# Who normalises the last two output tiles of a graph kernel's second layer norm: GpSimd and VectorE in place of ScalarE

## What is computed

```python
x = _layernorm(x + _L0_gnn_ref(x, adj, pairs, Wq, bq, Wk, bk), axis=-1)
x = _layernorm(x + _L1_gnn_ref(x, adj, weight, bias), axis=-1)   # adj @ (x @ weight) + bias

def _layernorm(x, axis=-1, eps=1e-05):
    m = jnp.mean(x, axis=axis, keepdims=True)
    v = jnp.var(x, axis=axis, keepdims=True)
    return (x - m) / jnp.sqrt(v + eps)
```

## Time and profile before

| what | value |
|---|---|
| median of 3 runs | 167.08 us (166.68 to 167.78) |
| profiled execution | 167.5 us, span 165.7 us |
| PE busy | 154.7 us (93%) |
| DVE busy | 125.5 us (76%) |
| ACT busy | 75.2 us (45%) |
| POOL busy | 69.2 us (42%) |
| TensorE granted clock, mean | 0.994 of full speed |

### The profile page before, as it was taken

How to read it: one execution, slowest core, us unless ns; L and a number is a source line. 1 busy time by engine, 2 the same in 40 slices (tenths; PEclk the granted TensorE clock), 3 DMA queues, 4 the chain that set the end, 5 groups by cost and what they waited for, 6 DMA issues and landing times.

```text
span 165.7 us, 2912 instructions
## 1 busy us (share of the span) xinstructions
PE 154.7 (93%) x1029; PEld 81.1 (49%) x1029; DVE 125.5 (76%) x391; ACT 75.2 (45%) x126; POOL 69.2 (42%) x83
## 2 busy tenths in 40 slices
PE   3999899999999999999999999998999999999950
PEld 3954344455444445444444485444655444444530
DVE  2885689996899998999578897888971268666681
ACT  5685649855864422874181362151213104342451
POOL 7787777777777777777107271000030000000000
PEclk9999999999999999999999999999999999999997
DMA  4999979998259999451004700000005962312233
GB/s 123 381 375 338 338 223 357 389 404 326 77 148 320 372 362 395 146 131 38 0 0 127 227 23 4 0 0 0 0 17 145 335 187 78 131 63 76 87 127 127
DMA packets 16232, 28.99 MB, mean 175 GB/s; under 512 B 4769, under 2 KB 5953, under 8 KB 16086
## 3 DMA queue, kind: packets, MB, share of 16 engines
q1 hardware_dynamic: 10742, 24.14, 41.6%
q10 hardware_dynamic: 3280, 3.07, 5.5%
q0 software_dynamic: 2192, 1.57, 3.8%
HBM read 19.83 MB, written 8.58 MB: 171 GB/s over the span
## 4 chain that ended last, share of the span: by engine, by line
PE 38%; DVE 24%; DMA 15%; issue 6%; ACT 6%; POOL 4%; SPq 3%; ACTq 0%; DVEq 0%
PE acc L1379 15%; PE acc L1467 13%; DMA stage<-in_adj_T 6%; DMA x_sb<-in_x 6%; POOL found L659 4%; DVE st L900 3%; PE tr L1467 3%; DMA found<-in_adj,top_i 3%; ACT adjT L702 2%; DVE hot L919 2%; DVE y L949 2%; PE tr L1421 2%; PE tr L1457 2%; SPq L546 1%; DVE x1s L963 1%
## 5 line engine op out<-in xcount | busy, mean ns | idle before, releaser
L651 POOL DMA_INDIRECT ed_adj<-in_adj,ed_idx x47 | 47.2, 1003 | 14.5 <-issue 14.0
L1379 PE MATMUL acc<-adjT,x1s 128*128 128x512 f16 (+1 forms) x240 | 49.0, 354 | 0.0
L1311 PE MATMUL acc<-xs,adjT 128*128 128x512 f16 (+1 forms) x176 | 40.2, 379 | 0.2 <-ACT xs L718 0.2
L1379 PEld LDWEIGHTS acc<-adjT,x1s 128*128 128x128 f16 x240 | 22.8, 98 | 21.0 <-issue 0.2
L1311 PEld LDWEIGHTS acc<-xs,adjT 128*128 128x128 f16 (+1 forms) x176 | 16.5, 98 | 19.2 <-ACT xs L718 0.7
L1467 PE MATMUL acc<-whl,xs 128*128 128x512 f16 (+1 forms) x108 | 23.8, 370 | 0.0
L1467 PEld LDWEIGHTS acc<-whl,xs 128*128 128x128 f16 x108 | 10.6, 98 | 11.8
L1311 PE MATMUL tr<-xs,adjT 128*128 128x512 f16 (+1 forms) x66 | 15.2, 379 | 0.0
L702 ACT CAST adjT<-stage 128x1408 f16<-128x1408 f32 x9 | 12.3, 1362 | 4.3 <-DMA stage<-in_adj_T 4.1
L755 ACT ACTIVATE xs<-acc 128x512 f16<-128x512 f32 (+1 forms) x12 | 6.4, 540 | 12.2 <-PE acc L1383 12.2
L690 POOL DMA_INDIRECT x_dram<-wraw,back_i x1 | 1.3, 1336 | 21.5 <-DVE wraw L1229 21.5
(11 more groups left out here) (279 smaller groups left out, 231.9 us busy)
## 6 DMA issues: line engine op xcount, KB each, us to landing
stage<-in_adj_T SPq DMA_DIRECT2D x9, 704.0 KB, 10.3
x_dram<-x_sb SPq DMA_DIRECT2D x10, 256.0 KB
x_sb<-in_x SPq DMA_DIRECT2D x3, 768.0 KB, 7.4
sums_dram<-y ACTq DMA_DIRECT2D x6, 256.0 KB
sums_dram<-xd ACTq DMA_DIRECT2D x5, 256.0 KB, 6.6
x_sb<-x_dram SPq DMA_DIRECT2D x1, 1280.0 KB, 12.3
out<-y SPq DMA_DIRECT2D x5, 256.0 KB, 2.0
stage<-in_adj_T SPq DMA_DIRECT2D x3, 384.0 KB, 5.8
```

The costliest lines, as they stand in the source:

```text
L651: nc.gpsimd.indirect_dma_start(out=ed_adj[0:EP, c:c + 1], out_offset=None, in_=adj_flat, in_offset=bass.IndirectOffsetOnAxis(ap=ed_idx[0:E ...
L1311: last = mm(sum_bank(i)[:, :], adjT[0:width[k], k, i * P:(i + 1) * P], xs[0:width[k], half, k, :], start=(k == 0 and half == 0), stop=(k = ...
L1379: mm(mix_bank(u)[:, 0:j - i], x1s[:, half, k, f * P:(f + 1) * P], adjT[:, k, i:j], start=(k == 0 and half == 0), stop=False)
```

## The change

Tile 9 is no longer normalised by ScalarE but by GpSimd, in one `tensor_scalar` over all 512 columns, as (y - mean) times the reciprocal. Tile 10 is normalised by VectorE alone, all 512 columns, in the same form. Neither needs the shift, so for these two tiles `scale_shift` gives way to `one_over`, a reciprocal alone. ScalarE still takes both roots, and still normalises tiles 0 to 8. The semaphores change with the work: SP waits for GpSimd before the DMA of tile 9, and both last DMAs wait for VectorE alone. The four buffers, the parts of the last tile and TensorE's program stay.

```diff
--- before.py
+++ after.py
@@ -40,7 +40,6 @@
 BACK_BEFORE = {0: 0, 1: 1, 5: 2, 6: 3}
 SPANS = [(0, 512), (512, 1024), (1024, N)]
 UNITS = KF * len(SPANS)
-HALF = H // 2
 LAST_PARTS = ((0, 320), (320, H))
 OUTS = 6
 EARLY = 2
@@ -253,7 +252,7 @@
         qk_read, change_ready, change_T, dT_hi, dT_lo = map(sem, ("qk_read", "change_ready", "change_T", "dT_hi", "dT_lo"))
         dS_done, right_hi, right_lo = map(sem, ("dS_done", "right_hi", "right_lo"))
         bias_row_loaded, bias_split, biased, ones_laid, out_done, z_ready, z_moments, z_root = map(sem, ("bias_row_loaded", "bias_split", "biased", "ones_laid", "out_done", "z_ready", "z_moments", "z_root"))
-        z_stats, z_normed, z_half_normed = map(sem, ("z_stats", "z_normed", "z_half_normed"))
+        z_stats, z_normed, next_to_last, next_to_last_normed, last_normed = map(sem, ("z_stats", "z_normed", "next_to_last", "next_to_last_normed", "last_normed"))
 
         map_clear, map_idx_ready, map_zeroed, map_marked = map(sem, ("map_clear", "map_idx_ready", "map_zeroed", "map_marked"))
         general_in, rows_in, general_step, early_read = map(sem, ("general_in", "rows_in", "general_step", "early_read"))
@@ -603,10 +602,12 @@
                     sp.dma_start(x_sb[0:LAST, a, :], rows(x1_dram, a)).then_inc(x1_back[n], 16)
             unless_few(sp, "sp", slots_wanted(sp), ahead, general_sp)
             for n, t in enumerate(OUT_ORDER[:-1]):
-                sp.wait_ge(z_normed, n + 1)
+                if n < T - 2:
+                    sp.wait_ge(z_normed, n + 1)
+                else:
+                    sp.wait_ge(next_to_last_normed, 1)
                 sp.dma_start(rows(out, t), y4(n)[0:width[t]]).then_inc(out_stored[n % 4], 16)
-            sp.wait_ge(z_normed, T)
-            sp.wait_ge(z_half_normed, 1)
+            sp.wait_ge(last_normed, 1)
             sp.dma_start(rows(out, OUT_ORDER[-1])[0:64, :], y4(T - 1)[0:64, :]).then_inc(last_stored[0], 16)
             for b in range(4):
                 sp.wait_ge(out_stored[b], 16 * len(range(b, T - 1, 4)))
@@ -692,6 +693,9 @@
                 in_=q[0:SLOTS, :], in_offset=None, bounds_check=N - 1, oob_is_err=False).then_inc(x1_scattered, 16)
             pool.wait_ge(x1_scattered, 16)
             unless_few(pool, "pool", slots_wanted(pool), ahead, general_pool)
+            t = T - 2
+            pool.wait_ge(next_to_last, 1)
+            nc.gpsimd.tensor_scalar(y4(t), y4(t), st[:, t % 2, 6:7], st[:, t % 2, 8:9], ALU.subtract, ALU.mult).then_inc(next_to_last_normed, 1)
 
 
         @block.scalar
@@ -807,12 +811,11 @@
             for t in range(T):
                 act.wait_ge(z_moments, t + 1)
                 root(st[:, t % 2], eps[:]).then_inc(z_root, 1)
-                act.wait_ge(z_stats, t + 1)
-                part = y4(t) if t < T - 1 else y4(t)[:, 0:HALF]
-                nc.scalar.activation(part, part, ACT.Identity, bias=st[:, t % 2, 9:10],
-                                     scale=st[:, t % 2, 8:9]).then_inc(z_normed, 1)
-            act.wait_ge(z_normed, T)
-            act.wait_ge(z_half_normed, 1)
+                if t < T - 2:
+                    act.wait_ge(z_stats, t + 1)
+                    nc.scalar.activation(y4(t), y4(t), ACT.Identity, bias=st[:, t % 2, 9:10],
+                                         scale=st[:, t % 2, 8:9]).then_inc(z_normed, 1)
+            act.wait_ge(last_normed, 1)
             act.dma_start(rows(out, OUT_ORDER[-1])[64:P, :], y4(T - 1)[64:P, :]).then_inc(last_stored[1], 16)
 
 
@@ -904,6 +907,10 @@
 
                 step(V.reciprocal(s[:, 8:9], s[:, 10:11]))
                 return V.tensor_scalar(s[:, 9:10], s[:, 6:7], -1.0, s[:, 8:9], ALU.mult, ALU.mult)
+
+            def one_over(s):
+
+                return V.reciprocal(s[:, 8:9], s[:, 10:11])
 
             def hot_part(n):
 
@@ -1273,14 +1280,14 @@
                 if n == 0:
                     ins.then_inc(dve_step, 1)
                     steps += 1
-                    finish_stats(T - 2)
+                    dve.wait_ge(z_root, T - 1)
+                    one_over(st[:, (T - 2) % 2]).then_inc(next_to_last, 1)
             step(ins)
             dve.wait_ge(z_normed, t - 1)
             V.bn_aggr(st[:, t % 2, 6:8], last_st[:, 0:12]).then_inc(z_moments, 1)
-            finish_stats(t)
-            dve.wait_ge(z_stats, T)
-            part = y4(t)[:, HALF:H]
-            V.tensor_scalar(part, part, st[:, t % 2, 8:9], st[:, t % 2, 9:10], ALU.mult, ALU.add).then_inc(z_half_normed, 1)
+            dve.wait_ge(z_root, T)
+            step(one_over(st[:, t % 2]))
+            V.tensor_scalar(y4(t), y4(t), st[:, t % 2, 6:7], st[:, t % 2, 8:9], ALU.subtract, ALU.mult).then_inc(last_normed, 1)
 
 
         @block.tensor
```

## The result

The changed kernel takes **169.7 us** (median of 6 runs, 168.61 to 170.63) against 166.96 us of the kernel before in the same measurement (median of 6, 166.68 to 167.78). The ratio is 1.0128, 95% interval [1.0084, 1.0172]: it is slower, by about 2.1 us by this ratio, which is clear of no change and still under 2%. The two medians alone lie further apart, 2.7 us, on six runs each. The prediction had said 167.4, with a range to 168.1. The profiled execution took 169.9 us with a span of 168.1, against 167.5 and 165.7.

The account below looks back on a forecast made before the run. TensorE, then a serial output tail, bounds the kernel. The output path gains 0.55 us, but GpSimd's end at 160.84 plus 5.05 of DRAIN and 0.2 gives span 166.1, +0.35: 167.4 us, range 166.2 to 168.1.

Parts of the forecast that it names:

- What bounds the kernel now: End of kernel: TensorE sets the pace until 159.6 us, then a serial 6 us tail for tiles 9 and 10.
- Output path, steps 1 to 3: Tiles 9 and 10 on VectorE: shifts go, 512 columns take 0.55 us, last DMAs at 161.98; gain 0.55 us.
- Step 4: Output DMAs: 1 us of room between tile 9's transfer and the last ones; output path alone ends the span at 165.15.
- GpSimd's instruction: Tile 9's normalisation on GpSimd: 0.8 us, ending at 160.84 (bounds 160.6 to 161.35).
- The hand-over: From the end of VectorE's reciprocal of tile 9 to GpSimd's start: 0.1 us, so start at 160.04.
- The drain: GpSimd's last DRAIN costs its own 5.05 us behind tile 9, ending at 165.89; span 166.1, +0.35 us; chance 0.48.
- The lock: VectorE and GpSimd's shared ports: VectorE's last normalisation is held only if GpSimd's instruction takes over 1.37 us.
- the third one: GpSimd's arithmetic needs several passes, 2.6 us, and its DRAIN follows whole: 169.3 us; chance of slow GpSimd 0.06.
- The drain costs little by 161: GpSimd's DRAIN at the end is short, so the output path decides: 166.5 us; chance 0.33.
- nothing moves: Last output DMAs land no earlier, their writes held by something unseen: about 167.1 us; chance 0.08.

Follow-up runs that it names:

- the probe: Kernel before plus six GpSimd instructions on unused scratch behind its branch, each waiting for the one ahead; one execution, 168.45 us.
- the wait alone: Kernel before with GpSimd waiting, ahead of its last DRAIN, for VectorE's last instruction, nothing else changed; 169.51 us, ratio 1.0115.
- the two with the early DRAIN: Changed kernel with a second GpSimd DRAIN ahead of the new instruction, 167.56 us; the same with SP issuing its half of tile 10 before tile 9, 167.35 us.
- both probes beside VectorE: Kernel before plus GpSimd instructions on unused scratch while VectorE works on other scratch, in two versions; one run each, 168.52 and 173.03 us.

## Why the prediction was wrong, step by step

*What bounds the kernel now.* It held. The tail is serial, and nothing of the change reaches ahead of it.

*Output path, steps 1 to 3.* They held to 0.01 us up to ScalarE's DMA at 161.98, counted from tile 9's reciprocal. VectorE's 512 columns took 0.55. Without GpSimd, and so with tile 9's shift kept, the path gives what was summed for it, 0.3 us. *Step 4* failed on SP's side, because GpSimd's end came late: SP's half of tile 10 went at 162.81 in the prediction's time instead of 161.98. Its 1 us of room was also too hopeful: with one operation on GpSimd both halves went 0.5 us earlier than before, tile 9's DMA 0.4 ahead of them, and SP's drain came 0.4 earlier, not 0.5.

*GpSimd's instruction.* **This is the step that failed.** The prediction took 0.8 us, between bounds of 0.58 and 1.31, all from rows of a cast and a select, "since both operations work on one read of the tile". It measured 2.36: 2.08 of its own and 0.28 from VectorE beside it. Even the upper bound was wrong. A data movement's price for a column was doubled to bound two arithmetic operations, and nothing in the trace of before priced arithmetic on GpSimd. The other half of the choice, to go by the row that is nearest in kind, had no row to go by, and that should have widened the range. The start of 0.05 us for an instruction came from no row either; the probe shows 0.36. The hand-over of 0.1 held: GpSimd started at 160.05 in the prediction's time, against 160.04.

*The drain.* It held, in mechanism and size. (Its sum is loosely rounded: 166.09 less 165.7 is 0.39, which gives 167.5 and not 167.4.) Put 2.36 in the place of 0.80 and the prediction's own sum reads: GpSimd ends at 162.40, the DRAIN at 167.4, the span at 167.65, which is +1.95 us or 169.0. The tail grew by 1.9, the time by the ratio of 1.0128 by 2.1 (1.4 to 2.9). The reason given for it, that the cost is the DRAIN's own and not the tail of something else, was shown by the wait alone, which costs 2.0 us of tail with no instruction behind it. The counter-evidence, ScalarE's 0.65 and SP's 0.007, concerned hardware queues and told nothing of GpSimd's.

*The lock.* The sum left it out because an instruction under 1.37 us would be over in time. That reason failed with the 2.36, and leaving it out was right by luck: VectorE's last instruction wasn't held although GpSimd ran until 162.91. It took 0.55 from 161.90, in the middle of GpSimd's run. The rule of the Trainium skill (SBUF — State Buffer, Who interferes with whom), that the second to come waits for the whole instruction, is not what these runs show beside a tensor_scalar of GpSimd; what they show is a loss of about 0.3 us on GpSimd's side and at most some tenths on VectorE's. Beside a GpSimd copy they do show the stall. The Trainium skill's 769 ns for a 512-element loop (GPSIMD Engine Reference, Elementwise — side-by-side cycle accounting) was no guide to this instruction: it took 2.08 alone.

*The rivals.* What happened is the third one, GpSimd slow with its drain whole (2.6 us, 169.3), to which the prediction gave 0.06. "The drain costs little by 161" was wrong; "nothing moves" too.

*The range* ended at 168.1 because it left that rival out.

## What to carry to other kernels

An engine that is idle early may still owe something at the program's end. Read its DRAIN in the profile before giving it late work: here 60 software DMAs left GpSimd 5 us of DRAIN, about 0.08 each by one execution, free at 126 us and on the critical path at 163; a DRAIN of its own in an idle stretch takes it off. Don't price arithmetic on GpSimd from its copies: two operations on 512 columns cost 2.1 us where a copy costs 0.6 and VectorE does the arithmetic in 0.55. And where several DMAs end a kernel, mind the last issue and what is issued just ahead of it, not the one that was made earlier.

## What the runs showed of the hardware that was not expected

- GpSimd's DRAIN behind 60 software DMAs: 4.97 to 5.06 us in nine profiles, and the same whether it begins at 126, 161 or 164 us; behind 5 software DMAs 0.53; behind none, with an earlier DRAIN, 0.1 past the instruction ahead.
- GpSimd's tensor_scalar, 128 partitions x 512 float32: two operations 2.08 us, one 1.56, two with constants 1.93; copy 0.61.
- Beside VectorE the two-operation form took 2.35 to 2.36 each time (in the changed kernel, in the two with the early DRAIN, and in both probes beside VectorE), whether VectorE ran one tensor_scalar there or five; the one-operation form in the changed kernel's place took 1.58, as alone.
- VectorE's L1132, 1.80 us in the earlier trace rows, takes 0.68 in the changed kernel, where GpSimd's cast starts later. Over all fourteen profiles it took 1.79 to 1.80 in the six where the cast began 0.15 us or more ahead of it, and 0.68 in the eight where it began ahead of the cast or within 0.01 us of it; there the cast took 1.47 to 1.85, and the next one of the same size 1.31. So the stall comes and goes between executions with which of the two is first.
